# Three steps moved in ScalarE's hand-written order: the first q/k copy, the residual's x, and the values' copy

## What is computed

```python
def attn(x):                              # x: (8, 512, 128), already layer-normed
    xn = rms_norm(x, ln1_w)
    q, k, v = xn @ Wq, xn @ Wk, xn @ Wv   # 16 heads of 8
    q, k = q * rsqrt(sum(q*q) + eps), k * rsqrt(sum(k*k) + eps)
    attn = softmax(mask((q @ k.T + bias) * scale)) @ v
    y = attn @ Wo + x
    return relu(rms_norm(y, ln2_w) @ W1) @ W2 + y

def moe(x):                               # 8 experts, top 2, inner width 352
    w = top2(softmax(x @ router.T))
    return sum over e of w[e] * ((silu(x @ gate[e].T) * (x @ up[e].T)) @ down[e].T)

x = x + layernorm(attn(layernorm(x)))
x = x + layernorm(moe(layernorm(x)))
```

## Time and profile before

| | |
|---|---|
| median of 3 runs | 597.91 us (597.78 to 597.98) |
| the profiled execution | 596.54 us |
| its span in the profile | 594.8 us |
| TensorE busy | 529.3 us, 89% of the span |
| ScalarE busy | 396.9 us, 67% |
| VectorE busy | 376.3 us, 63% |
| GpSimd busy | 348.5 us, 59% |
| mean granted TensorE clock | 0.98 of full speed |

### The profile page before, as it was taken

The page is one execution under the profiler, slowest core; times in us unless marked ns, Lnnn a source line. Parts: engine busy times, 40 slices in busy tenths (PEclk is TensorE's granted clock), DMA queues, the critical chain, the costliest instruction groups (busy, mean ns, idle before and its releaser), DMA issues.

```text
span 594.8 us, 14582 instructions
## 1 busy us (share of the span) xinstructions
PE 529.3 (89%) x4947; PEld 387.8 (65%) x4947; DVE 376.3 (63%) x1087; ACT 396.9 (67%) x884; POOL 348.5 (59%) x453
## 2 busy tenths in 40 slices
PE   6989899999899899998899899999886699999980
PEld 4655456556566446655555666889886699999930
DVE  6824583965975946996947786637752365555247
ACT  3488989888978788859788786644542355555425
POOL 6103636545538885357877358488678755465534
PEclk9999999999999999999999999999997899999986
DMA  7346323213214322222734511212222213321174
GB/s 196 77 128 160 111 93 110 71 46 108 80 37 130 103 76 82 76 96 79 203 104 139 137 56 46 65 51 64 56 64 66 65 34 90 83 67 33 33 283 142
DMA packets 47016, 55.62 MB, mean 94 GB/s; under 512 B 7376, under 2 KB 41056, under 8 KB 44784
## 3 DMA queue, kind: packets, MB, share of 16 engines
q1 hardware_dynamic: 42624, 45.76, 27.0%
q0 software_dynamic: 4320, 8.92, 4.6%
HBM read 36.27 MB, written 18.92 MB: 93 GB/s over the span
## 4 chain that ended last, share of the span: by engine, by line
PE 56%; DVE 15%; ACT 9%; POOL 6%; issue 5%; another core or an unknown queue 4%; DMA 3%; DVEq 1%; SPq 0%; ACTq 0%; POOLq 0%
PE SC L862 11%; PE OA L739 9%; PE OA L872 6%; PE M L777 4%; PE M L813 4%; PE SC L721 3%; ACT arena L1006 3%; PE SC L725 2%; PE M L634 2%; DVE SS L1322 2%; PE SC L731 2%; PE M L653 2%; POOL slots L1752 1%; PE M L843 1%
## 5 line engine op out<-in xcount | busy, mean ns | idle before, releaser
L1006 ACT ACTIVATE arena<-SC 128x1024 f32<-128x1024 f32 x160 | 161.9, 1038 | 14.6 <-PE SC L726 11.8
L862 PE MATMUL SC<-arena 128*128 128x128 f32 (+1 forms) x852 | 108.9, 279 | 0.0
L862 PEld LDWEIGHTS SC<-arena 128*128 128x128 f32 (+1 forms) x852 | 101.6, 187 | 0.4 <-issue 0.3
L739 PE MATMUL OA<-arena 128*32 128x256 f32 (+1 forms) x1536 | 88.9, 349 | 6.6 <-DVE arena L446 2.8
L1752 POOL DMA_INDIRECT slots<-XBA,IDX x64 | 72.8, 1138 | 37.0 <-DVE IDX L1447 19.6
L1495 DVE TENSOR_TENSOR arena<-arena,SC 128x256 f32<-128x256 f32 (+1 forms) x142 | 43.6, 348 | 64.0 <-issue 22.3
L872 PE MATMUL OA<-arena 128*128 (+1 forms) x426 | 62.0, 283 | 13.5 <-issue 7.6
L739 PEld LDWEIGHTS OA<-arena 128*32 128x32 f32 x1536 | 39.3, 109 | 44.0 <-issue 22.9
L872 PEld LDWEIGHTS OA<-arena 128*128 128x128 f32 (+1 forms) x426 | 54.4, 195 | 16.2 <-issue 16.2
L445 POOL TENSOR_TENSOR arena<-arena 128x512 f32<-128x512 f32 x32 | 42.7, 1335 | 36.2 <-ACT arena L1006 35.6
L438 POOL TENSOR_TENSOR arena<-arena 128x512 f32<-128x512 f32 x23 | 31.2, 1356 | 48.9 <-ACT arena L1006 48.9
(11 more groups left out here) (254 smaller groups left out, 1086.1 us busy)
## 6 DMA issues: line engine op xcount, KB each, us to landing
arena<-parts SPq DMA_DIRECT2D x90, 192.0 KB
parts<-arena SPq DMA_DIRECT2D x16, 384.0 KB, 3.0
arena<-ytok SPq DMA_DIRECT2D x8, 512.0 KB, 6.6
XGA<-slots SPq DMA_DIRECT2D x39, 65.0 KB
arena<-slots SPq DMA_DIRECT2D x32, 65.0 KB
X<-in_L_attn_x SPq DMA_DIRECT2D x4, 512.0 KB, 5.2
out<-X SPq DMA_DIRECT2D x8, 256.0 KB, 2.4
arena<-parts SPq DMA_DIRECT2D x12, 96.0 KB
```

Source lines behind the costliest of these rows:

```text
L739: mm = pe.matmul(OA[32 * j:32 * j + 32, q0:q0 + n], vals[:, t, 32 * h:32 * h + 32], probs(j), start=first, stop=last, skip_group_check=True)
L862: mm = pe.matmul(SC[0:n, r % 2, 512 * m + P * c:512 * m + P * (c + 1)], WSEL[s % 4][:, I * m + i0:I * m + i0 + n], XGT[r % 2], start=True, ...
L1006: act.activation(EB[u], SC[:, n % 2, :], ACT.Exp).then_inc(exp_done, 1)
```

## The change

In ScalarE's table the first q/k copy goes from unit 15 to unit 16 (`qk0=-5` to `-4`) and the values' copy from unit 2 to unit 3 (`val=2` to `3`). Within a unit the residual's x is now tested ahead of the seeds; both have unit 1, so in bodies 1 to 6 x now comes first. In unit 3 the values stand behind the unit's exponential and ahead of the doubling of the rows (L1203). No instruction is added or taken away.

```diff
-ACT_AT = (dict(val=2, seed=1, xt=-6, qk0=-5, qk1=-2, out0=12, out1=1, rx=2, ...
+ACT_AT = (dict(val=3, seed=1, xt=-6, qk0=-4, qk1=-2, out0=12, out1=1, rx=2, ...
...
                     if b == 0 and n in TABLE_AT:
                         exp_table(TABS // 2 + TABLE_AT.index(n))
+                    if 1 <= b <= NB:
+                        c = b - 1
+                        if n == at["xa"]:
+                            xa(c)
                     if 1 <= due(PRE["seed"], b, n) < NB:
                         root_seeds(due(PRE["seed"], b, n))
...
                     for k, name in enumerate(("xt", "qk0", "qk1")):
                         if 2 <= due(PRE[name], b, n) < NB:
                             pre_copy(due(PRE[name], b, n), k)
-                    if 1 <= b <= NB:
-                        c = b - 1
-                        if n == at["xa"]:
-                            xa(c)
                     if b < NB and n == at["out0"]:
                         out_bank(b, 0)
```

More of the change, by code:

```diff
@@ L44 @@
     dict(rx=0, logits=1, vsum=0, count=3, o0=1, o1=2, yt=3, wo=5, zt=6, h0=7, h1=7, h2=7, h3=7, ffn_a=8, ffn=8))
-ACT_AT = (dict(val=2, seed=1, xt=-6, qk0=-5, qk1=-2, out0=12, out1=1, rx=2, rexp=6, yt=4, ysq=12, zt=7, h0=8, h1=9, h2=10, h3=10, xb2=3, part0=4, half0=4, last0=6, part1=8, half1=9, last1=10, xar=-7, xa=1),
+ACT_AT = (dict(val=3, seed=1, xt=-6, qk0=-4, qk1=-2, out0=12, out1=1, rx=2, rexp=6, yt=4, ysq=12, zt=7, h0=8, h1=9, h2=10, h3=10, xb2=3, part0=4, half0=4, last0=6, part1=8, half1=9, last1=10, xar=-7, xa=1),
     dict(out1=0, rx=0, xb2=2, rexp=3, yt=4, zt=6, ysq=6, h0=6, h1=6, h2=7, h3=7, xa=3))
```

## The result

The changed kernel took **602.53 us** (median of 6 runs, 599.97 to 606.32), the kernel before on the same chip 597.94 (6 runs, 594.99 to 599.13): ratio 1.0078, 95% interval 1.0050 to 1.0106. It is 4.6 us slower; 594.7 was forecast. The profiled execution of the changed kernel took 601.92, its span is 600.2.

A forecast was written before the change was run, and what follows sets the result against it. No engine sets the pace alone; gains exist only where TensorE waits, at six hand-overs between bodies. Terms 0.90 + 0.55 + 0.85 + 0.90 = 3.2 us, set against the median 597.91, give 594.7; range 590.5 to 597.4.

The forecast's parts named there:

- values copied in unit 3: From hand-over 1/2 on, five places: XBT comes 0.53 us sooner behind exponential 3; the values' delay costs nothing.
- the cover: Bank M0, unit 4: XBT still lies some 0.6 ahead of the transposes at 1/2; without this, up to 0.5 lost.
- First q/k copy later: Six hand-overs: exponential 16 runs before the copy, saving 0.90 us each on ScalarE, 5.4 at most.
- The term of 0/1: Hand-over from body 0 to 1: full gain of 0.90 us, no L1602 group and no XBT there yet.
- The collision in L1602: Hand-overs 1/2, 2/3, 4/5: GpSimd's earlier L438 costs VectorE about 1.15 us, made good at L1614; VectorE's gain about 0.
- 1/2, 2/3 and 4/5: Hand-overs between these bodies: 1/2 gives only the values' share, 0.55 us; 2/3 and 4/5 give 0.
- The terms of 3/4 and 5/6: Hand-overs where VectorE does unit 16's multiply: gains of 0.85 and 0.90 us, capped by transposes at most 0.9 sooner.
- Residual's x ahead of the seeds: Bodies 1 to 6: 1.6 us of work fits the wait where sums are late; elsewhere later seeds cost nothing.
- The slower one: Rival: GpSimd's operations in a row hold a VectorE multiply 2.5 us in bodies 3 and 5; 602 us, chance 0.07.
- no collision: Rival: VectorE keeps its run of short operations, GpSimd comes after; 5.3 us less, 592.6, chance 0.25.
- all waits back: Rival: waits of 5.9 and 5.1 us all come back at six hand-overs; 11.0 less, 586.9, chance 0.08.
- swallowed: Rival: gain ends in masks, scatters, or last bodies' and first expert tiles' waits; within 1.2 us, 597.5, chance 0.13.

The follow-up runs named there:

- val_only: Only the values' copy moved to unit 3, against the kernel before: 605.9 us where that took 597.8, ratio 1.0124.
- qk_only: Only the first q/k copy moved to unit 16, against the kernel before: 599.0 us where that took 597.8, ratio 1.0011.
- xa_g3: Kernel before with x ahead of the seeds, and VectorE's L1372 waiting for GpSimd's L446 in bodies 4 and 6: 596.1 us against 594.5, ratio 0.9997.
- before_g3: Kernel before plus one wait: VectorE's L1372 waits for GpSimd's L446 in bodies 4 and 6; 596.7 us against 594.5, ratio 1.0036.
- xa_b: Second profile of the kernel before with only x moved ahead of the seeds: stretch 331.0 (first profile 338.0); timed 598.9 us against 596.3.
- all_g13: Whole change plus waits of GpSimd's unit-3 multiply for L1342 and VectorE's L1372 for L446 (bodies 4, 6), against kernel before: 595.9 us against 596.3, ratio 1.0048.

## Why the prediction was wrong

**The step that failed is "values copied in unit 3", costed at nothing.** I asked only who waits for the values (L666, bank M0), and there the cover held: L666 never waited for L1028. But swapping them with exponential 3 also brings exponential 3 sooner, and that exponential releases GpSimd's L445 of unit 3. Before, it started as L1342 ended; now it starts inside it (119.18 in a group from 118.51 to 121.03). What the runs show in place of nothing: 1.1 of VectorE's time at three places, 2.0 to 3.1 of TensorE's wait before L666 in all (the four profiles with the values moved and no guard), in val_only both first ties lost, and 8.1 us by the medians for this step alone. With both guards it costs nothing against the guarded kernel before. That the two engines exclude each other stood in my own text, and I used it for exponentials 16 and 18 only.

**First q/k copy later.** The wait of 5.9 fell to 0.7 as forecast. The term of 0/1 was right for this step: 0.91 to 0.92 in each of the four profiles with the q/k copy moved and the values not, for a forecast 0.90. With the values moved as well it is 1.37 to 1.38: they gave 0.44 there in val_only, for which the forecast had no term. The collision in L1602 (1.01 longer, forecast 1.15), made good at L1614, came as predicted, and so did 1/2, 2/3 and 4/5 giving nothing of it: in qk_only they cost about 0.26 each. The terms of 3/4 and 5/6 (0.85 and 0.90) did not arrive. At 3/4 qk_only gained 0.27, and at 5/6 it lost 0.76, with a clock fall. TensorE's waits for exponentials before L725 were gone, but it waited more before L721 and before L739. I priced these waits as time and did not ask what two pauses close together do to its clock.

**Residual's x ahead of the seeds.** "Costs nothing" holds for what the seeds feed (xa_g3 level with before_g3; xa_b's stretch 331.0), but not for the tie: with x moved VectorE wins it, 4 times of 4. That is +2.6 by the medians (1.0064 by the ratio), nothing in one profile and 6.5 us of stretch in the other. I had read both rows, L1372 at 0.97 and L446 starting 0.14 behind it, and saw a held row, not a race that 0.1 us can turn.

**The rivals.** The slower one, at 0.07 and 602, has the right time by luck and half of the right mechanism. The lasting collisions were 1.1 each, close to its 1.15, but in L1342 and not in L1602, and at 1/2 as well. The hold of several operations in a row came the other way round: VectorE's operations held a GpSimd multiply for 2.95 us, not in bodies 3 and 5 but in 4 and 6, and part of the time went through the second tie and the clock, which it did not have. What the Trainium skill (SBUF — State Buffer, "Who interferes with whom") says of the shared ports, read as a hold for one instruction, fails in this direction too: L446 of GpSimd, asked for at 206.87, stood behind five VectorE instructions, the last of them L1355 until 209.23. The other three cases (no collision, all waits back, swallowed) are out.

**The sum for the changed kernel.** Its stretch is 4.4 and 7.5 longer than the kernel before's in two profiles, with 1.7 and 6.8 us of clock lost inside it; 3.3 of VectorE's collisions and one long second tie (1.3, in the first of them) are the rest, overlapping. By the table above it ends 3.7 and 6.0 behind; the measured 4.6 lies between. A split to the tenth cannot be given: falls and ties differ from execution to execution. How near the forecast was without them is an estimate: all_g13 is 0.8 slower than the kernel before by the means and loses 5.0 more of clock, at 0.7 to 0.95 us for each; without that loss it would be 2.7 to 4 us faster, for a forecast 3.2.

## What to carry to other kernels

When an instruction is moved on an engine, ask of each neighbour that it passes who is released sooner, not only who gets it later; with VectorE and GpSimd both near full use, a release that moves by half a microsecond can land inside the other's group. Before moving anything, look for places where two engines ask within 0.2 us of each other: a kernel that wins them in every profile has something to lose. A wait as a guard can hold an order that a change would break (here one wait took the collision away and brought back more than half of the loss), but it moves what stands behind it, and cost 2.2 us where the order was right anyway. And read the granted clock beside the waits, in the timed runs as well as in a profile: two short pauses of TensorE pushed together can cost more than both did apart, and one profile cannot tell whether they will.

## What the runs showed of the hardware that was not expected

- A GpSimd multiply asked for while VectorE had five instructions without a gap ahead of it took 2.92 to 2.95 us in place of 0.73, in eleven of twelve cases. In the twelfth (qk_only, body 6) VectorE stood idle for 0.27 after three of them, GpSimd came in there, and it took 1.65. The reverse, GpSimd holding VectorE for several operations, was in the earlier trace rows with 2.96; the longest here is 5.83 (xa_b, L446 at 214.07, while GpSimd ran five multiplies in a row until 219.61).
- VectorE's L1378 reads one operand from a PSUM bank and one from SBUF. In bodies 4 and 6, where GpSimd scatters, it starts 0.04 after L804 in 22 of 40 cases and 0.46 to 1.94 after it in 18. In bodies 1, 2, 7 and 8, where no scatter runs at that moment, it is 0.04 in all 80. In four of the five long cases without a guard it began within 0.07 us of the end of a scatter, but with the guard it began in the middle of one (214.16, in a scatter from 213.94 to 214.89). So the delay goes with the scatters, and what holds L1378 is open; no run takes the scatters away.
- The same program with the same offsets to 0.01 us went either way at the second tie, with 1.2 us between the outcomes and the clock fall behind it.
- TensorE's granted clock fell to 0.50 for 3.4 us behind pauses of 1 to 2 us in total, 0 to 4 times in the stretch, and even in the same program differently (1 and 4 times in the changed kernel, 2 and 0 with x alone). Behind one pause of 1.28 us that all twenty profiles share it fell in four, and L1378 of body 1 then came 1.4 to 1.6 us later. What exactly lets it fall stays open.
- The kernel before took 588 to 604 us in some sets and 579 to 588 in others. In its profiles (596.5, and 578.9 and 583.6) the difference is all behind 430 us, in the experts' tiles: the stretch agrees to 0.2. That it is the chip is not shown: chip 12 is named for a set with a median of 596.3 and for the two shorter profiles alike.
